# A graph layer and a mixture of experts on one core: the sums of the message passing kept feature by node

## The reference

```python
def gnn(feat, row, col, val, W1, b1, W2, b2, eps, offset, scale):
    aggr = segment_sum(val[:, None] * feat[col], row, N)
    aggr = aggr + (1.0 + eps) * feat
    h = relu(relu(aggr @ W1 + b1) @ W2 + b2)
    return (h - mean(h)) * scale * rsqrt(var(h) + 1e-10) + offset
x = x + gnn(layernorm(x), src, dst, edge_weight, ...)
x = x + ffn(layernorm(x), ...)   # router, softmax, top 2 of 8 experts:
                                 # gelu(xe @ W1 + b1) @ W2 + b2, weighted sum
```

## Time and profile before

| | |
|---|---|
| time, median of 3 runs | 1289.24 us (1284.93 to 1290.47) |
| profiled execution, time and span | 1288.74 us, 1286.8 us |
| PE matmuls busy | 901.3 us (70%) |
| PE weight loads busy | 615.4 us (48%) |
| DVE busy | 733.5 us (57%) |
| ACT busy | 677.3 us (53%) |
| POOL busy | 670.6 us (52%) |

### The profile page before, as it was taken

One profiled execution on the slowest core, in us unless ns is written; L12 is line 12 of the kernel. 1 busy time (PEld: TensorE's weight loads), 2 busy tenths in 40 slices (PEclk: granted clock), 3 DMA queues, 4 the chain that ended last, 5 costly groups with the idle time before them and its releaser, 6 DMA issues.

```text
span 1286.8 us, 25490 instructions
## 1 busy us (share of the span) xinstructions
PE 901.3 (70%) x6921; PEld 615.4 (48%) x6922; DVE 733.5 (57%) x1645; ACT 677.3 (53%) x2181; POOL 670.6 (52%) x678
## 2 busy tenths in 40 slices
PE   2383487548765476564677767686279999999995
PEld 1131232225332233232465645575167778787883
DVE  4664286548655474454564564887835555555553
ACT  7894398219873178752233332463245555555552
POOL 3836356752676626666457647322434544544542
PEclk9985599669776688865676678796589999999998
DMA  4114222332233313333244432173012223223222
GB/s 121 61 47 140 58 62 87 95 84 69 83 90 95 92 38 94 89 103 112 62 131 148 124 119 92 54 212 130 2 58 40 43 48 49 45 45 49 46 45 25
DMA packets 59608, 102.47 MB, mean 80 GB/s; under 512 B 10298, under 2 KB 43048, under 8 KB 59400
## 3 DMA queue, kind: packets, MB, share of 16 engines
q0 software_dynamic: 29520, 65.96, 21.1%
q1 hardware_dynamic: 30008, 35.55, 8.7%
HBM read 84.27 MB, written 17.20 MB: 79 GB/s over the span
## 4 chain that ended last, share of the span: by engine, by line
PE 42%; DVE 16%; ACT 11%; issue 10%; another core or an unknown queue 6%; DMA 2%; DVEq 2%; POOL 1%; POOLq 0%; ACTq 0%
PE bank L999 7%; ACT Wall L1085 7%; PE bank L985 4%; PE bank L987 4%; PE bank L986 4%; ACT RB L1093 4%; PE bank L843 3%; PE bank L1001 3%; PE bank L841 3%; DVE RA L1564 3%; PE bank L854 3%; PE bank L842 2%; DVE Wall L1564 2%; PE bank L806 2%
## 5 line engine op out<-in xcount | busy, mean ns | idle before, releaser
L675 POOL DMA_INDIRECT Wall<-xl_d,gbuf x391 | 392.4, 1004 | 292.1 <-PE bank L843 137.6
L1093 ACT ACTIVATE RB<-RB,gbuf 128x128 f16<-128x128 f16 x488 | 178.9, 424 | 301.9 <-DVE RB L1551 208.7
L841 PE MATMUL bank<-Wall,RB 128*128 x488 | 167.7, 344 | 155.6 <-DVE Wall L1564 54.4
L1085 ACT ACTIVATE Wall<-Wall 128x128 f32<-128x128 f16 (+1 forms) x782 | 246.9, 383 | 24.8 <-DVE Wall L1482 16.8
L1564 DVE TENSOR_TENSOR RA<-RA,bank 128x256 f32 x244 | 102.0, 418 | 269.3 <-remote 143.2
L1205 ACT ACTIVATE RA<-bank,b1T 128x128 f32<-128x128 f32 x448 | 128.1, 369 | 120.9 <-PE bank L987 120.8
L734 POOL DMA_INDIRECT out_dram<-RA,slot_tok x56 | 101.1, 1805 | 160.8 <-ACT RA L1211 143.0
L806 PE MATMUL bank<-Wall 128*128 128x512 f16 (+1 forms) x391 | 154.7, 444 | 33.9 <-ACT Wall L1085 20.8
L985 PE MATMUL bank<-RA,Wall 128*128 128x128 f16 x896 | 175.4, 221 | 0.3 <-issue 0.3
L987 PE MATMUL bank<-RA,Wall 128*128 128x128 f16 x896 | 175.4, 221 | 0.0
L986 PE MATMUL bank<-RA,Wall 128*128 128x128 f16 x896 | 175.3, 221 | 0.0
(11 more groups left out here) (314 smaller groups left out, 1584.3 us busy)
## 6 DMA issues: line engine op xcount, KB each, us to landing
stage<-in_L_ffn_W SPq DMA_DIRECT2D x10, 1024.0 KB
Wall<-xl_d,gbuf POOLq DMA_INDIRECT x391
Wall<-in_L_ffn_W SPq DMA_DIRECT2D x6, 1024.0 KB, 6.6
Wall<-in_x SPq DMA_DIRECT2D x4, 640.0 KB, 6.7
xl_d<-Wall SPq DMA_DIRECT2D x4, 640.0 KB
out_dram<-RB SPq DMA_DIRECT2D x4, 640.0 KB
xn_d<-RA SPq DMA_DIRECT2D x4, 640.0 KB
RB<-in_x SPq DMA_DIRECT2D x1, 1792.0 KB
```

The lines of the kernel that those rows point to most:

```text
L675: pool.indirect_dma_start(out=ring[:, t % RING * 2 * D:(t % RING + 1) * 2 * D], out_offset=None, in_=xl_d, in_offset=bass.IndirectOffsetOn ...
L841: mm(o, high, ring[:, bass.ds(at, D)], start=True, stop=False)
L1085: last = act.activation(hi_word[:, n % SR, k * S:(k + 1) * S], hi_hot[:, n // HB % 2, n % HB // 2, 0:S, n % 2], ACT.Copy, scale=pay[k][:, ...
L1093: act.activation(low, high, ACT.Copy, scale=rec_r[:, n:n + 1]).then_inc(sw_built, 1)
```

## The change

The sums are kept feature by node instead of node by feature. In a step the gathered rows are now the weights and the masks stream: for each half of the features (`kc`) there are three matmuls of 128 columns, high rows × high mask, high rows × low mask, low rows × high mask. So a step has six matmuls and six weight loads, and the address of the weights is dynamic. The addition on DVE has the same size.

The own parts must be turned too. PE does it in the sort of chunk 0 (`turn_rows`): 13 pairs of tiles, eight fp16 matmuls a pair with an fp16 identity (`ident_h`, a new copy on POOL at the start) as the moving operand, four for the last, into the banks that the steps use later. DVE scales each pair from the bank into `acc_odd` (`own_sums`, at columns 40, 48, 56, 64 and 72 of the sort) in place of the five operations L1539. SP's loads and DVE's start of the steps wait for these 13.

In the MLP the two transposes, ACT's copy and `aggT` are gone: the product with gw1 reads `acc` itself, when POOL's sum of the tile is there. The factor `w_back` is put into gw1 by one ACT operation ahead of the MLP. The product with gw2 alternates between banks 0 and 4. In the diff the unchanged lines between the edits are left out; `weights` is a helper of the kernel that makes a weight operand from a dynamic byte address.

```diff
+        RING_AT = 2 * (2 * w2f - RING * D)
...
-        aggT, h1T, xT = ([rec_all[:, (2 * k + q) * D:(2 * k + q + 1) * D] for q in range(2)] for k in range(3))
+        h1T, xT = ([rec_all[:, (2 * k + q) * D:(2 * k + q + 1) * D] for q in range(2)] for k in (1, 2))
+        ident_h = sb("ident_h", [P, P], F16)
...
+        def own_out(p):
+            return bank[1 + p % 3][:, 0:min(2, NT - 2 * p) * D]
+        def h2_out(t):
+            return bank[4 * (t % 2)][:, 0:D]
+        PAIRS = (NT + 1) // 2
+        turned_behind = lambda p: 33 + 3 * p
...
-            sp.wait_ge(acc_set, NT // G)
+            sp.wait_ge(acc_set, PAIRS)
...
+            pool.tensor_copy(ident_h[:, :], ident[:, :])
...
-                return (words[h] // RING ** k) % RING * (2 * D)
+                return (words[h] // RING ** k) % RING * (4 * D)
...
-                o = agg_out(n)
-                mm(o, high, ring[:, bass.ds(at, D)], start=True, stop=False)
-                mm(o, low, ring[:, bass.ds(at, D)], start=False, stop=False)
-                mm(o, high, ring[:, bass.ds(at + D, D)], start=False, stop=True).then_inc(agg_mm, 1)
+                for kc in range(KC):
+                    o = agg_out(n)[:, kc * P:(kc + 1) * P]
+                    row_high, row_low = (weights(at, RING_AT + k * D + kc * P, P) for k in range(2))
+                    mm(o, row_high, high, start=True, stop=False)
+                    mm(o, row_high, low, start=False, stop=False)
+                    m = mm(o, row_low, high, start=False, stop=True)
+                m.then_inc(agg_mm, 1)
...
+            def turn_rows(p):
+                tiles = range(2 * p, min(2 * p + 2, NT))
+                pe.wait_ge(xl_done, tiles[-1] + 1)
+                if p >= 3:
+                    pe.wait_ge(acc_set, p - 2)
+                for k, t in enumerate(tiles):
+                    for kc in range(KC):
+                        o = own_out(p)[:, (k * KC + kc) * P:(k * KC + kc + 1) * P]
+                        mm(o, x_parts[:, t, kc * P:(kc + 1) * P], ident_h[:, :], start=True, stop=False)
+                        m = mm(o, x_parts[:, t, D + kc * P:D + (kc + 1) * P], ident_h[:, :], start=False, stop=True)
+                m.then_inc(x_turned, 1)
+            p = 0
+                if p < PAIRS and turned_behind(p) == i:
+                    turn_rows(p)
+                    p += 1
+            assert p == PAIRS
...
-            for n in range(-2, NT + 2 * G + 3):
-                t = n + 2
-                if 0 <= t < NT:
-                    if t >= 2:
-                        pe.wait_ge(t_out, t - 1)
-                    pe.wait_ge(acc_sum, t + 1)
-                    for kc in range(KC):
-                        m = nc.tensor.transpose(bank[t % 2][:, kc * P:kc * P + P], acc[:, t, kc * P:kc * P + P], ident[:, :])
-                    m.then_inc(t_mm, 1)
+            pe.wait_ge(gw1_scaled, 1)
+            for n in range(-1, NT + 2 * G + 3):
...
-                    pe.wait_ge(t_out, t + 1)
+                    pe.wait_ge(acc_sum, t + 1)
-                                   aggT[t % 2][:, kc * P:kc * P + P], start=kc == 0, stop=kc == KC - 1)
+                                   acc[:, t, kc * P:kc * P + P], start=kc == 0, stop=kc == KC - 1)
-                    if t >= 1:
-                        pe.wait_ge(h2_relu, t)
-                    mm(bank[4][:, 0:D], one_b[:, :], gb2_rows, start=True, stop=False)
+                    if t >= 2:
+                        pe.wait_ge(h2_relu, t - 1)
+                    mm(h2_out(t), one_b[:, :], gb2_rows, start=True, stop=False)
-                        m = mm(bank[4][:, 0:D], h1T[t % 2][:, kc * P:kc * P + P], gw2[:, kc, :],
+                        m = mm(h2_out(t), h1T[t % 2][:, kc * P:kc * P + P], gw2[:, kc, :],
...
+            act.wait_ge(mlp_in, 80)
+            act.activation(gw1, gw1, ACT.Copy, scale=w_back[:, 0:1]).then_inc(gw1_scaled, 1)
-            for n in range(-2, NT + 2 * G + 3):
-                t = n + 2
-                if 0 <= t < NT:
-                    act.wait_ge(t_mm, t + 1)
-                    if t >= 2:
-                        act.wait_ge(h1_mm, t - 1)
-                    act.activation(aggT[t % 2], bank[t % 2][:, 0:D], ACT.Copy, scale=w_back[:, 0:1]).then_inc(t_out, 1)
+            for n in range(-1, NT + 2 * G + 3):
...
-                    act.activation(h2[:, t, :], bank[4][:, 0:D], ACT.Relu).then_inc(h2_relu, 1)
+                    act.activation(h2[:, t, :], h2_out(t), ACT.Relu).then_inc(h2_relu, 1)
...
+            def own_sums(n):
+                for p in range(PAIRS):
+                    if n - HB <= turned_behind(p) < n:
+                        if p == 0:
+                            dve.wait_ge(eps_ready, 1)
+                        dve.wait_ge(x_turned, p + 1)
+                        o = own_out(p)
+                        at = 2 * p * D
+                        dve.tensor_scalar(acc_odd[:, at:at + o.shape[1]], o, eps1[:, 0:1], None, ALU.mult).then_inc(acc_set, 1)
...
+                if n % HB == 0 and n > turned_behind(0):
+                    own_sums(n)
-            dve.wait_ge(eps_ready, 1)
-            for g in range(NT // G):
-                rows = slice(G * g, G * (g + 1))
-                dve.tensor_scalar(x_in[:, rows, :], x_in[:, rows, :], eps1[:, 0:1], None, ALU.mult).then_inc(acc_set, 1)
...
-            dve.wait_ge(acc_set, NT // G)
+            dve.wait_ge(acc_set, PAIRS)
```

More of the change, by code:

```diff
@@ L358, in moe_gnn_program @@
         acc_zeroed = sem("acc_zeroed")
+        x_turned = sem("x_turned")
+        gw1_scaled = sem("gw1_scaled")
         acc_sum = sem("acc_sum")
@@ L384, in moe_gnn_program @@
         mlp_in = sem("mlp_in")
-        t_mm = sem("t_mm")
-        t_out = sem("t_out")
         h1_mm = sem("h1_mm")
```

## The result

The changed kernel takes 1313.42 us in the median (four runs, 1308.95 to 1315.54), the kernel before 1287.09 beside it: ratio 1.0202, 95% interval 1.0165 to 1.0238. It is slower by some 26 us. My 1293 was 20 us too low; the range of 1264 to 1325 held it, but that range was wide enough for a gain as well as for a loss. The time lies in the interval of rival A (slower, 1308 to 1338), to which I had given a chance of 0.23.

The account below looks back on a forecast made before the run. The prediction saw no single engine bounding the whole: ACT limited the first sort, signals the steps, DVE the MLP's end. Steps +4, their start +1, own parts +2, MLP −3 made +4 on 1288.74: 1293 us, range 1264 to 1325.

Parts of the forecast that it names:

- rival A: In the steps, the doubled PE instruction stream becomes the limit: 1308 to 1338 us, 1315 as middle; chance 0.23.
- signs of being right: Six starts in 0.28–0.32 us; steps within 10 us of 668; MLP's DVE waiting until about 810; first gather 103–107.
- part 3: MLP without transposes and ACT copy: PE's gain shows only between 811 and 845, −3 us, bounds 0 and −12.
- signs of being wrong: PE issue before inner matmuls; 20 steps before 140 or remote well under 143; pitch 0.08; L1085 gap over 3 us.
- Rival B: First steps' stall (131 to 149) goes: −18 us in place of +1, 1274 or 1270 in all; chance 0.33.
- rival C: In the steps, load and matmul pairs come at 81 instead of 56 ns: +30 to +40 us, 1325; chance 0.05.
- Part 1, the array: In the steps, six 128-column matmuls take the array time of three 256-column ones: 3 us, 0.5 by chain share.
- Part 1, the sequencer: In the steps, doubled loads, matmuls and addresses cost PE's sequencer +4 us, a fifth of the 20 us upper bound.
- part 2: Own parts turned in the sort of chunk 0: +2 us, bounds −1.7 and +3.5; PE's turns at no cost.
- Start of the steps: First steps: x's load issued some 12 us earlier, ahead of the first gather; +1 us, bounds −18 and +6.
- my own range: Whole kernel, likeliest case: 1284 to 1302 us, −9 if the MLP gives all, +9 if half the steps' bound comes.

Follow-up runs that it names:

- agg_back2: The changed kernel with the old step of three 256-column matmuls, masks as weights, on a 1157 us chip: 1160.60 us, 1.0034 of the kernel before.
- after2: The changed kernel itself, unaltered, run again on a 1157 us chip: 1171.78 us, 1.0124 of the kernel before.
- agg_back: The changed kernel with the old step of three 256-column matmuls, masks as weights, on a 1290 us chip: 1301.18 us, 1.0037 of the kernel before.
- split_masks: The kernel before with each step's three matmuls cut into six of 128 columns, masks still weights, on a 1290 us chip: 1323.59 us, 1.0229.
- static_rows: The changed kernel with ring slots known when built, so no address operations on PE, on a 1290 us chip: 1310.20 us, 1.0110 of the kernel before.
- no_low_rows: The changed kernel without the high rows by low mask product, so four matmuls a step, on a 1290 us chip: 1316.40 us, 1.0161 of the kernel before.
- turns_back: The changed kernel without PE's 100 turning matmuls, DVE's 13 scalings kept but reading memory, on a 1157 us chip: 1160.42 us, 1.0027 of the kernel before.
- split2: The kernel before with each step's three matmuls cut into six of 128 columns, masks still weights, on a 1157 us chip: 1174.05 us, 1.0152.
- pool_scale: The kernel before with the five own-part scalings on POOL instead of DVE, on a 1157 us chip: 1168.94 us, 1.0104.
- sums_back: The changed kernel with PE's turns kept but DVE's five old scalings back in their place, on a 1157 us chip: 1168.87 us, 1.0098 of the kernel before.
- paced_start: The kernel before with POOL's gathers 8 to 31 each made to wait for the step eight before, on a 1157 us chip: 1157.51 us, 0.9997.
- act_scale: The kernel before with own parts scaled on ACT, DVE's first masks ahead of its wait for them, on a 1157 us chip: 1158.32 us, 1.0010.
- experiment 7: The kernel before with own-part scalings moved off DVE: on POOL 1168.94 us, 1.0104; on ACT 1158.32 us, 1.0010.

## Why the forecast was right in its range and wrong in its size

**The signs.** Of the four signs of being right one came: DVE in the MLP still waits for POOL, until about as long behind the last step as before (33 us, see part 3). The steps are 20 us from 668 and not within 10, the first gather comes at 110.49 and not by 107, and a step's six starts span 0.34 us in the median, just over 0.32. Of the signs of being wrong A's came: the "issue" ahead of the two inner matmul lines went from 4.2 and 3.7 us to 7.5 and 7.9 (L859 and L860). B's and C's didn't, and ACT's longest gap was 2.26 us, under the 3 that I had named, while its four gaps together made 5.6.

**Part 1, the array.** "The array is no gain and no loss" held: most pairs stand 0.056 to 0.06 us apart at full clock and 0.107 at the low one. The 81 ns of the Trainium skill, "TensorE: Matmul & The Clock Gate", section "Back-to-back issue gap" (rival C), were not the pitch of any step at full clock.

**Part 1, the sequencer: this is the step that was mis-sized.** I had put +4 where 21 came on the 1290 us chips and 11 on a 1157 us chip. The term was 488 × 0.28 × 0.15, and a fifth of that. The 0.28 us assumed every pair at 0.11; only one gap of a step is that long. But long gaps and slow clock come on top of it: from the first start to the last matmul's end all steps together took 330.9 us before and 379.0 after, +48, which is 0.10 us a step, 0.35 of the bound and not a fifth. On a 1157 us chip they took 298.6 (`agg_back2`) and 319.8 (`after2`), +21, 0.16 of the bound. Of these 48 and 21 us, 21.1 and 11.2 came out in the time, a share of 0.44 and 0.53, where I had taken 0.15, what lines L841 to L843 hold of the chain. A step's end also stands behind pieces of the chain that carry other names ("issue" 10%, "another core or an unknown queue" 6%), and DVE's additions already waited 106.3 us for L843.

But one half is no constant either, as the profiled executions show:

| kernel | matmuls a step | all steps in sum | steps, first to last start | ratio |
|---|---|---|---|---|
| 1290 us chips | | | | |
| before | 3 | 330.9 | 666.8 | 1 |
| `agg_back` | 3 | 326.7 | 672.0 | 1.0037 |
| after | 6 | 379.0 | 687.9 | 1.0202 |
| `split_masks` | 6 | 367.8 | 699.6 | 1.0229 |
| `static_rows` | 6 | 349.2 | 687.7 | 1.0110 |
| `no_low_rows` | 4 | 302.6 | 693.9 | 1.0161 |
| 1157 us chips | | | | |
| `agg_back2` | 3 | 298.6 | 536.1 | 1.0034 |
| `after2` | 6 | 319.8 | 548.8 | 1.0124 |
| `turns_back` | 6 | 320.5 | 544.6 | 1.0027 |
| `split2` | 6 | 328.4 | 548.8 | 1.0152 |

`split_masks` adds 37 us to the steps and about 30 to the time, `static_rows` takes 30 off the changed kernel's steps and some 12 off the time, `no_low_rows` takes 76 off and some 5. So the six matmuls are shown to be the cause, by taking them out (`agg_back`) and by putting them in alone (`split_masks`, `split2`); a rule that turns a step's length into time is not shown.

**Part 1, the delivery (rival A).** Its case came, but not as I priced it (steps of 6.3 us each), and that the time lies near the middle of its interval is luck: part 2's 6.6 us are in it, which the rival did not have, and a 1157 us chip shows a loss of 15 us without any late instruction. The long gaps within steps grew by 28.3 − 8.5 = 20 us, spread over the run in pieces of mostly 0.5 to 2.1 us. That the step costs 10 us more on the chip with such gaps than on the one without agrees with this at a share of one half; that the gaps are the whole difference is worked out, not shown by a run. The Trainium skill, "Runtime: NRT & Kernel Launch", section "Instruction fetch mechanics", calls the cost of crossing a block "mostly hidden". On the 1157 us chips the traces agree (no gap above 0.4 us within a step); on the 1290 us chips there are such gaps, but no row ties them to a crossing, so the case doesn't decide it.

**A term I didn't have: the clock.** The granted clock over the steps went from 0.73 to 0.69, and 58% of the steps end at the low level instead of 46% (in the kernel before, a matmul of 256 columns shown longer than 0.35 us). My estimate from these rows: without its long gaps a step of the changed kernel takes 0.566 us in the mean at the high level and 0.827 at the low one (before 0.510 and 0.833). So of the 48 us some 20 are long gaps, some 15 are steps that moved to the low level, and some 13 are the longer step itself. On the 1157 us chip 34% end at the low level in both kernels, and the 21 us are all of the last kind. How much of the time each of these makes was not separated.

**Start of the steps.** I had +1. The load of x is issued at 106.00 now, 3 us earlier and not 12, but ahead of the first gather at 110.49 as I had put it. The first 32 steps took 74.6 us against 69.9, +4.7, inside the bound of +6. Rival B failed on the 1290 us chips. On the others a part of it is seen: the first 32 steps take 41 to 44 us in the four kernels whose load of x comes ahead of the gathers (`after2`, `agg_back2`, `turns_back`, and 43.6 in `pool_scale`), and 46 in the four where it doesn't (`sums_back`, `paced_start`, `split2`, `act_scale`). Step 33 begins at 154.5 in `after2` and at 155.3 in `split2`, so a first step that comes 4 us later costs nothing there. No run moves that load alone.

**Part 2.** +2 forecast, +6.6 measured (first step), outside the bound of +3.5. My own terms give +4.5 and not +3.5 when none of the 4.2 comes back (1.8 and 2.7 lost), which is still too little. The single costs were near (0.69 us a scaling against the 0.6 taken; ACT starves where DVE's masks are late), though the 64 operations of ACT's run are 32 columns and not 64. The failing sentence is "spread over the whole sort it follows ACT, no cost taken" for PE's turns: they wait for DVE's scalings, and DVE's masks for the sort matmuls behind them (ACT's gaps on L1508: 0.25, 2.26, 1.06 and 1.98 us). I summed two engines' work without drawing the circle.

**Part 3.** −3 forecast, −1.4 read, and over all runs too small to be told from the spread: from the last step to the end, seven kernels with the new MLP took 507.9 to 509.6 us and an eighth 512.3, six with the old one 508.6 to 512.4. The mechanism was right. DVE's line in the changed kernel:

```profile
820.92 16.01 DVE L1410 TENSOR_TENSOR lnt<-small 128x5 f32<-128x5 f32 x1
```

DVE reaches it 16.8 us behind the last step's last matmul (820.9 − 804.1) instead of 20.9 (797.3 − 776.4), 4.1 earlier, and it then stands 16.01 us instead of 12.76, until 836.9, which is when POOL's sums and offsets end.

**The range.** The upper end of my own range had "+9 if half of part 1's bound comes", but half of 20 us in place of 4 is +6, so it should have read 1299. The measured time lies above either.

## What to carry to other kernels

Cutting matmuls into twice as many of half the width was free for the array here and not for the engine's instruction side. Count instructions and address operations a step, and don't weigh them by the share that the matmul lines hold of the chain: it gave 0.15 where 0.44 and 0.53 came. When work is put into idle time of two engines that already wait for each other, draw the circle of waits: apart, the two halves moved the first step by 0.4 and 1.8 us (`sums_back`, `turns_back`, against `split2`), and together by 4.0 (`after2`). Don't take a price from one chip to another, or add up the prices of parts, without a run that shows it. Before a stage is relieved, look for the engine that ends it (POOL in the MLP here), or the gain is only a longer wait.

## What the hardware showed that I had not expected

- The kernel before takes 1157 us on two chips and 1287 to 1297 on others, the changed one 1171.8 and 1313.4, and nearly all of the difference lies in the steps: 672.0 against 536.1 us for the same kernel (`agg_back`, `agg_back2`). On the 1290 us chips DVE is told of matmul ends late (143 us of "remote") and PE's instructions come 0.5 to 2.1 us apart now and then. On the others there is next to none of either (3.3 us of "remote" in `agg_back2`), though POOL's runs of gathers with 0.3 us between them are longer: up to 112 in a row in `after2`, 32 in the kernel before and in the changed one. Runs of gathers are therefore no sufficient cause; what differs between the chips stays open.
- POOL's five operations of 1280 f32 values took 17.5 us, and five of DVE's operations beside them were held for about 3 us each (experiment 7): this work on POOL was not free for DVE, though the two share no data there.
- With a third fewer matmuls in the steps the granted clock over them fell from 0.69 to 0.63 (`no_low_rows`).
